# A recurrence on one core: the gates' passes cut differently, and a bias put into PSUM by ScalarE

## The reference, cut to what matters

```python
def cell(h, x):
    gi = x @ W_ih + b_ih
    gh = h @ W_hh + b_hh
    i_r, i_z, i_n = jnp.split(gi, 3, axis=-1)
    h_r, h_z, h_n = jnp.split(gh, 3, axis=-1)
    r = jax.nn.sigmoid(i_r + h_r)
    z = jax.nn.sigmoid(i_z + h_z)
    n = jnp.tanh(i_n + r * h_n)
    h_new = (1.0 - z) * n + z * h
    return (h_new, h_new)
hs = jax.lax.scan(cell, cond_2048, x)
```

## Time and profile before

| | us |
|---|---|
| median of 3 runs | 4225.12 |
| lowest, highest | 4210.37, 4236.23 |
| profiled execution, span (first to last instruction) | 4227.2 |
| TensorE (PE) busy | 3809.6 (90%) |
| TensorE weight load (PEld) busy | 2500.0 (59%) |
| VectorE (DVE) busy | 2336.6 (55%) |
| ScalarE (ACT) busy | 1317.9 (31%) |
| GpSimd (POOL) busy | 520.7 (12%) |

### The profile page before, as it was taken

One profiled execution on the slowest core, in us unless ns is written; L12 is line 12 of the kernel. 1 busy time (PEld: TensorE's weight loads), 2 busy tenths in 40 slices (PEclk: granted clock), 3 DMA queues, 4 the chain that ended last, 5 costly groups with the idle time before them and its releaser, 6 DMA issues. The chain is left out here.

```text
span 4227.2 us, 169699 instructions
## 1 busy us (share of the span) xinstructions
PE 3809.6 (90%) x68983; PEld 2500.0 (59%) x68983; DVE 2336.6 (55%) x6671; ACT 1317.9 (31%) x4227; POOL 520.7 (12%) x1107
## 2 busy tenths in 40 slices
PE   7999999999999999998899999689999979688880
PEld 3888888888888888886344343244333334344440
DVE  2555555555555555555677777444666654222226
ACT  0333333333333333332344444223444421011110
POOL 0010000100010000100222222000000004411110
PEclk9999999999999999999999999799999989898995
DMA  4900000000000000010111110101111212166677
GB/s 120 369 19 0 0 0 0 0 0 0 0 0 0 0 0 0 0 30 30 40 53 42 44 52 18 73 30 53 52 52 52 71 41 88 50 215 223 229 229 280
DMA packets 144030, 270.20 MB, mean 64 GB/s; under 512 B 23273, under 2 KB 70517, under 8 KB 140002
## 3 DMA queue, kind: packets, MB, share of 16 engines
q1 hardware_dynamic: 109570, 194.03, 13.7%
q10 hardware_dynamic: 20992, 57.17, 4.1%
q0 software_dynamic: 13408, 18.20, 1.2%
HBM read 148.41 MB, written 89.39 MB: 56 GB/s over the span
## 5 line engine op out<-in xcount | busy, mean ns | idle before, releaser
L310 PE MATMUL gru_pr<-ahead,h 128*4 128x128 f32 x16384 | 558.3, 274 | 14.2 <-DVE h L414 14.2
L310 PE MATMUL gru_pz<-ahead,h 128*4 128x128 f32 x16384 | 542.0, 273 | 4.2 <-issue 4.2
L310 PE MATMUL gru_pn<-ahead,h 128*32 128x128 f32 x16384 | 543.5, 273 | 0.0
L310 PEld LDWEIGHTS gru_pn<-ahead,h 128*32 128x32 f32 x16384 | 460.1, 110 | 1.4
L310 PEld LDWEIGHTS gru_pz<-ahead,h 128*4 128x4 f32 x16384 | 439.3, 87 | 12.0 <-issue 4.8
L310 PEld LDWEIGHTS gru_pr<-ahead,h 128*4 128x4 f32 x16384 | 342.1, 88 | 156.0 <-DVE h L414 25.7
L356 ACT ACTIVATE gru_rn<-gru_pre 128x16 f32<-128x16 f32 x512 | 120.2, 235 | 682.3 <-DVE gru_pre L396 682.3
L394 DVE STREAM_TRANSPOSE gru_tr<-gru_pr 128x128 f32<-128x128 f32 x512 | 162.1, 317 | 291.4 <-PE gru_pr L310 291.4
L927 DVE TENSOR_REDUCE da_mx<-da_ps 128x2 f32<-128x1024 f32 (+3 forms) x256 | 201.2, 817 | 131.9 <-PE da_ps L620 131.9
L273 POOL COPY gru_pick<-ident 128x4 f32 x512 | 96.0, 187 | 1445.5 <-PE gru_pz L301 1439.7
L407 DVE STREAM_TRANSPOSE gru_tz<-gru_pz 128x32 f32<-128x32 f32 (+1 forms) x1024 | 195.2, 229 | 122.9 <-PE gru_pz L310 122.9
(11 more groups left out here) (295 smaller groups left out, 5598.0 us busy)
## 6 DMA issues: line engine op xcount, KB each, us to landing
ahead<-in_L_ffn_gate_up_proj SPq DMA_DIRECT2D x64, 768.0 KB, 4.8
yk<-gru_zeros SPq DMA_DIRECT2D x6, 4096.0 KB, 34.8
ex_wd<-in_L_ffn_down_proj ACTq DMA_DIRECT2D x64, 384.0 KB, 6.3
xg<-gru_zeros SPq DMA_DIRECT2D x4, 4224.0 KB, 30.7
ex_xg<-xg ACTq DMA_DIRECT2D x64, 264.0 KB, 5.8
ahead<-wide SPq DMA_DIRECT2D x15, 1024.0 KB, 4.7
ahead<-xnT SPq DMA_DIRECT2D x15, 1024.0 KB, 4.5
co_got<-yk SPq DMA_DIRECT2D x8, 1536.0 KB, 7.9
```

What stands on the lines that cost most here:

```text
L310: last = nc.tensor.matmul(rows(j), of(c), whh[:, c, g, j, :], start=(c == 0 and start), stop=(c == KD - 1))
```

## The change

The same sums are made in another cut. Pass one ("rz") forms r's 128 columns of each group and the first 32 of z's, 160 in one matmul, into a new PSUM tensor `prz` that replaces `pr`; pass two forms n; pass three forms z's other 96 columns into `pz`. The 32 columns are z for the first quarter of h. W_hh is therefore laid out with the three gates side by side for each quarter and group, loaded by 64 DMAs in pieces of 128 values.

The order on TensorE becomes: rz for c = 0; n for c = 0; then the wait for the rest of h; rz for c = 1 to 3; n for c = 1 to 3; z. z's input is added by four matmuls of 32 columns and four of 96. All of the steps' matmuls have start off: they add to what `add_z_input` put there, to zero bits (r), or to n's bias.

n's bias is multiplied once, ahead of the loop, and kept as `bias_rows`; in each step ScalarE copies it into PSUM (`pn`) after `gru_tn` has been read and ahead of tanh, and TensorE's n waits for that (`seeded`). VectorE transposes 160 columns for r and the z quarter together; ScalarE does that quarter's sigmoid right after r's. The rest of z is one transposition of 96 columns and one sigmoid. The two scans for h stay, behind that transposition in VectorE's order.

```diff
--- before.py
+++ after.py
@@ -95,13 +95,14 @@
                 sp.wait_ge(xT_psum, (b - 1) * KD)
                 sp.dma_start(xin[:, b % 2, :, :], x[b].rearrange("(tt p) d -> p tt d", p=P)).then_inc(x_in[b % 2], 16)
             sp.wait_ge(w_spread, 3 * KD)
-            whh = t.ahead[:].rearrange("p (c g j f) -> p c g j f", c=KD, g=3, j=KD)
+            whh = t.ahead[:].rearrange("p (c j g f) -> p c j g f", c=KD, g=3, j=KD)
             for jj in range(KD):
-                rows = W_hh.rearrange("(jj c i) n -> jj i c n", jj=KD, c=KD)[jj]
+                rows = W_hh.rearrange("(jj c i) (g j f) -> jj i c j g f", jj=KD, c=KD, g=3, j=KD)[jj]
                 for c in range(KD):
-                    sp.dma_start(whh[32 * jj:32 * jj + 32, c, :, :, :].rearrange("i g j f -> i (g j f)"), rows[:, c, :]).then_inc(whh_in, 16)
+                    for j in range(KD):
+                        sp.dma_start(whh[32 * jj:32 * jj + 32, c, j, :, :], rows[:, c, j, :, :]).then_inc(whh_in, 16)
             sp.wait_ge(hin_in, 16 * KD * KD)
-            sp.wait_ge(whh_in, 16 * KD * KD)
+            sp.wait_ge(whh_in, 16 * KD * KD * KD)
 
         @block.gpsimd
         def _(pool):
@@ -201,18 +202,19 @@
         def sb(name, shape):
             return ctx.enter_context(nc.sbuf_tensor("gru_" + name, shape, F32))
 
-        whh = t.ahead[:].rearrange("p (c g j f) -> p c g j f", c=KD, g=3, j=KD)
+        whh = t.ahead[:].rearrange("p (c j n) -> p c j n", c=KD, j=KD)
+        RZ, Z, N = slice(0, P + 32), slice(P + 32, 2 * P), slice(2 * P, 3 * P)
         wih = t.ahead2[:].rearrange("p (k n) -> p k n", k=KD)
         xT = t.wide[:].rearrange("p (k b t) -> p k b t", b=B, k=KD)
         NG, NBL = 2 * KD, T // 32
-        bias, one = sb("bias", [P, KD, P]), sb("one", [P, 8 * B])
-        tr, pre = sb("tr", [P, KD, 32]), sb("pre", [P, ST])
-        tn, tz, narg = sb("tn", [P, KD * 32]), sb("tz", [P, KD, 32]), sb("narg", [P, ST, 4])
+        bias, one, bias_rows = sb("bias", [P, KD, P]), sb("one", [P, 8 * B]), sb("bias_rows", [P, P])
+        tr, pre = sb("tr", [P, KD + 1, 32]), sb("pre", [P, ST])
+        tn, tz, narg = sb("tn", [P, KD * 32]), sb("tz", [P, KD - 1, 32]), sb("narg", [P, ST, 4])
         rn, zin, pick = sb("rn", [P, ST, 4]), sb("zin", [P, D]), sb("pick", [P, 2, B])
         d0, d1 = sb("d0", [P, ST, 4]), sb("d1", [P, ST, 4])
         zeros = sb("zeros", [P, 1, XW])
-        pr = ctx.enter_context(nc.psum_tensor("gru_pr", [P, 4 * P], F32))
         pn = ctx.enter_context(nc.psum_tensor("gru_pn", [P, 4 * P], F32))
+        prz = ctx.enter_context(nc.psum_tensor("gru_prz", [P, 4 * P], F32))
         pz = ctx.enter_context(nc.psum_tensor("gru_pz", [P, 2, 4 * P], F32))
         pgi = ctx.enter_context(nc.psum_tensor("gru_pgi", [P, 4 * P], F32))
         wst = sb("wst", [P, KD, P])
@@ -224,6 +226,7 @@
         r_rows, n_rows, z_rows = sem("r_rows"), sem("n_rows"), sem("z_rows")
         tr_done, pre_done, r_act = sem("tr_done"), sem("pre_done"), sem("r_act")
         tn_done, gin_ready, set_up, bias_set = sem("tn_done"), sem("gin_ready"), sem("set_up"), sem("bias_set")
+        opened, seeded = sem("opened"), sem("seeded")
         narg_done, tanh_done, tz_done, z_act = (sem(n) for n in ("narg_done", "tanh_done", "tz_done", "z_act"))
         block = ctx.enter_context(nc.Block())
         state = t.h[:, :, 6]
@@ -289,33 +292,44 @@
         def _(pe):
             pe.wait_ge(loaded, 16)
 
-            def add_bias(s):
-                pe.wait_ge(tn_done, s * 1 + 1)
-                for j in range(KD):
-                    nc.tensor.matmul(pn[32 * j:32 * j + 32, 0:P], one[:], bias[:, j, :], start=True, stop=False)
+            pe.wait_ge(tn_done, 1)
+            for j in range(KD):
+                last = nc.tensor.matmul(pn[32 * j:32 * j + 32, 0:P], one[:], bias[:, j, :], start=True, stop=True)
+            last.then_inc(opened, 1)
 
             def add_z_input(s, par):
                 pe.wait_ge(pick_ready, s * 1 + 1)
-                pe.wait_ge(tz_done, s * 2 + 2)
+                pe.wait_ge(tr_done, s * 1 + 1)
                 for j in range(KD):
-                    last = nc.tensor.matmul(pz[32 * j:32 * j + B, par, 0:P], pick[:, par, :], zin[:, j * P:(j + 1) * P],
-                                            start=True, stop=False)
+                    nc.tensor.matmul(prz[32 * j:32 * j + B, P:P + 32], pick[:, par, :], zin[:, j * P:j * P + 32],
+                                     start=True, stop=True)
+                pe.wait_ge(tz_done, s * 1 + 1)
+                for j in range(KD):
+                    last = nc.tensor.matmul(pz[32 * j:32 * j + B, par, 0:P - 32], pick[:, par, :], zin[:, j * P + 32:(j + 1) * P],
+                                            start=True, stop=True)
                 last.then_inc(z_added, 1)
 
-            def gate(rows, g, of, start, done, s=None):
-                for c in range(KD):
-                    if s is not None and c < 2:
-                        pe.wait_ge(h_ready, s * 2 + (c + 1))
+            def part(rows, of, cols, cs, done=None):
+                for c in cs:
                     for j in range(KD):
-                        last = nc.tensor.matmul(rows(j), of(c), whh[:, c, g, j, :], start=(c == 0 and start), stop=(c == KD - 1))
-                last.then_inc(done, 1)
+                        last = nc.tensor.matmul(rows(j), of(c), whh[:, c, j, cols], start=False, stop=True,
+                                                skip_group_check=True)
+                if done is not None:
+                    last.then_inc(done, 1)
 
             def step(s, par):
                 after = lambda c: t.h[:, c * B:(c + 1) * B, 6]
                 places = lambda c: t.h[:, c * B:(c + 1) * B, :].rearrange("p b x -> p (b x)")
-                gate(lambda j: pr[32 * j:32 * j + B, 0:P], 0, after, True, r_rows, s)
-                gate(lambda j: pn[32 * j:32 * j + 32, 0:P], 2, places, False, n_rows)
-                gate(lambda j: pz[32 * j:32 * j + B, par, 0:P], 1, after, False, z_rows)
+                rz_rows = lambda j: prz[32 * j:32 * j + B, RZ]
+                n_of = lambda j: pn[32 * j:32 * j + 32, 0:P]
+                pe.wait_ge(h_ready, s * 2 + 1)
+                part(rz_rows, after, RZ, (0,))
+                pe.wait_ge(seeded, s * 1 + 1)
+                part(n_of, places, N, (0,))
+                pe.wait_ge(h_ready, s * 2 + 2)
+                part(rz_rows, after, RZ, (1, 2, 3), r_rows)
+                part(n_of, places, N, (1, 2, 3), n_rows)
+                part(lambda j: pz[32 * j:32 * j + B, par, 0:P - 32], after, Z, range(KD), z_rows)
 
             def next_gate_input(kb, c, k):
                 if k == 0:
@@ -331,14 +345,12 @@
                     for k in range(KD):
                         s = kb * 32 + c * KD + k
                         add_z_input(s, k % 2)
-                        add_bias(s)
                         next_gate_input(kb, c, k)
                         step(s, k % 2)
             with pe.Fori(T // 2 - 16, T // 2) as q:
                 for par in range(2):
                     s = q * 2 + par
                     add_z_input(s, par)
-                    add_bias(s)
                     step(s, par)
 
         @block.scalar
@@ -354,11 +366,13 @@
                 nc.scalar.activation(d0[:, :, 1], state, ACT.Copy).then_inc(h_copied, 1)
                 act.wait_ge(pre_done, s * 1 + 1)
                 nc.scalar.activation(rn[:, :, 2], pre[:], ACT.Sigmoid).then_inc(r_act, 1)
+                nc.scalar.activation(d1[:, 0:B, 2], tr[:, KD, 0:B], ACT.Sigmoid).then_inc(z_act, 1)
+                act.wait_ge(tn_done, s * 1 + 2)
+                nc.scalar.activation(pn[:, 0:P], bias_rows[:], ACT.Copy).then_inc(seeded, 1)
                 act.wait_ge(narg_done, s * 1 + 1)
                 nc.scalar.activation(d0[:, :, 2:4], narg[:, :, 3:4].broadcast_to([P, ST, 2]), ACT.Tanh).then_inc(tanh_done, 1)
-                for n, part in enumerate(PARTS):
-                    act.wait_ge(tz_done, s * 2 + (4 + n + 1))
-                    nc.scalar.activation(cb(d1[:, part.start * B:part.stop * B, 2]), tz[:, part, 0:B], ACT.Sigmoid).then_inc(z_act, 1)
+                act.wait_ge(tz_done, s * 1 + 3)
+                nc.scalar.activation(cb(d1[:, B:ST, 2]), tz[:, :, 0:B], ACT.Sigmoid).then_inc(z_act, 1)
 
             with act.Fori(0, NBL) as kb:
                 with act.Fori(0, 32) as n:
@@ -371,8 +385,8 @@
             dve.wait_ge(bias_set, 2)
             nc.vector.memset(one[0:1, 6:8 * B:8], 1.0).then_inc(bias_set, 1)
 
-            nc.vector.memset(pr[:], 0.0)
             nc.vector.memset(pn[:], 0.0)
+            nc.vector.memset(prz[:], 0.0)
             nc.vector.memset(pz[:], 0.0)
@@ -383,17 +397,21 @@
             nc.vector.memset(d1[:, :, 3], 1.0).then_inc(set_up, 1)
             dve.wait_ge(set_up, 6)
             dve.sem_inc(tn_done, 1)
-            dve.sem_inc(tz_done, 4)
+            dve.sem_inc(tz_done, 2)
+            dve.sem_inc(tr_done, 1)
```

(13 more changed lines are left out.)

## The result

The kernel after takes 4244.66 us (median of 9 runs, 4239.52 to 4252.03), the kernel before on the same chips 4226.39 (median of 9, 4210.37 to 4245.55). The ratio is 1.0035, 95% interval 1.0021 to 1.005: slightly slower, inside the 1% that the prediction called no change. The forecast was 4147, some 79 us faster; the kernel is 18 slower. The range (4102 to 4260) holds the time.

What follows compares the result with a forecast made beforehand. Each 3.64 us step was bound by z's chain, nearly tied with TensorE's tail. 392 steps x 0.21 = 82, less 120 x 0.03 = 4, gave about 79 us off: 4147, range 4102 to 4260.

Steps and rivals of the forecast that it cites:

- Part 4: z's 96 columns: rows at 2.81, first h scan at 3.18 after tanh and transposition, step 3.43, gain 0.21 us.
- Part 3: n's rows at 2.15, its transposition to 2.55, scan of tanh's argument at 2.59, tanh 2.91 to 3.15 us.
- What a record costs: Four-record TensorE waves follow a straight line in columns: 0.136 us for 160, 0.0825 for 96, 0.03 for 32.
- Rival A: TensorE's narrow waves do not shrink, so the change is slower: 4263 to 4302 us; chance 0.18.
- Part 1: rz first: TensorE has 0.49 us of work before needing the rest of h, so the 0.03 stall goes.
- Part 2: r's rows at 1.49 us instead of 1.09, their transposition to 1.91, r's sigmoid 2.27 to 2.50.
- Part 5: Rest of h reaches TensorE 0.33 us into the next step, under 0.49 of work: hidden.
- Part 6: Bias leaves TensorE's tail (2 waves, 0.22 us), z's input takes 4 waves; TensorE free at 3.35, under 3.43.
- Part 7: ScalarE's copy into PSUM ahead of tanh costs 0, since tanh could start at 2.84, under 2.91 us; 0.1 for the range.
- Part 9: Loading W_hh in 64 DMAs takes 32 us to issue, ending by 57, before the first step at 105.0.
- Part 8: The 120 steps after a loop's branch, held by TensorE's sequencer, take 3.67 us, a loss of 0.03 each.
- B: Another tie eats the gain, through costly 32-column input waves and late tanh: 4197 us; chance 0.22 with the rest of another rival.

Runs made afterwards that it cites:

- bias_multiplied: both_waits with n's bias multiplied on TensorE in every step and no ScalarE copy: 4223.95 us, 0.9996 of the kernel before.
- copy_one_column: both_waits with ScalarE's copy of n's bias cut to one of its 128 columns: 4148.85 us, 0.9824 of the kernel before.
- both_waits: Kernel after, first h scan waiting for tanh alone and tanh's argument scan carrying the wait for n's transposition: 4151.88 us, 0.9818 of the kernel before.
- value_first: Kernel after with tanh's wait moved behind that for z's first sigmoid, none dropped: 4211.39 us, 0.9969 of the kernel before.
- before_z_detached: Kernel before with an always fulfilled wait added ahead of the first h scan's wait for z's sigmoid: 4250.93 us, 1.005 of the kernel before.
- tensor_unrolled: both_waits with TensorE's inner loop over 8 steps instead of 4: 4504.71 us, 1.0661 of the kernel before.

## Why the prediction was wrong

The mechanism that it named for the gain is there. What failed is a term of the sum: two hand-overs on VectorE, in parts 4 and 3, were priced at 0.03 and 0.04, and measured 0.20 and 0.13.

- *What bounds the kernel before*: right. z's chain ended last and TensorE's tail all but tied with it; bias_multiplied shows the tie as soon as VectorE is quicker.
- *What a record costs*: right. By the line, 96 columns were to take 0.0825 a wave and 160 columns 0.136; z's 32 records take 0.84 less one record's 0.25 and the rest of its wave's 0.02, 0.57 for 7 waves, 0.082 each. The prediction's own sign, 0.66 for the 8 waves, came out too: z's first matmul starts at 1003.00, that of z's input at 1003.66. The four waves of z's input shrank too. The Trainium skill's 25 ns between starts of matmuls (TensorE: Matmul & The Clock Gate, "Wait — 56ns, not 53.3ns?") does not hold for the four records of a wave: at 0.10 a wave these 7 would have taken 0.70, and the two 32-column waves of z's input 0.20, where its 96-column matmuls start 0.06 behind them (1003.66 to 1003.72). Rival A fell with it.
- *Parts 1, 2, 5, 6, 7, 9*: right. h's rest came under the quarter's work, ScalarE's copy is free (copy_one_column), and the tail fits: 2.96 + 0.41 = 3.37 in both_waits, by L338's load at 1007.29, where 3.35 was forecast. W_hh's 64 DMAs took 43.88 us to issue and not 32, and were still done by 68.3, ahead of the first step. The timeline of SP's queue, kernel after:

```profile
24.43 43.88 SPq L103 DMA_DIRECT2D ahead<-in_L_cond_W_hh  x64
```

- *Part 3, the step that failed first*: "narg 2.59" came at 2.67. It took the distance from n's transposition to the scan, 0.03 to 0.04, from the step of the kernel before, where that wait was carried and r's sigmoid had ended 0.28 earlier. In the kernel after the wait is not carried, which gives 0.13. Even where it is again, the scan starts only after 0.06.
- *Part 4, the step that failed most*: "Scan of the first quarter after tanh and tz: 3.18" came at 3.42. It reckoned the scan as ready when its last input was, and priced the hand-over at that of a carried wait. That hand-over was measured in the kernel before on z's sigmoid; tanh, which now came last, had a wait of another kind. Measured: 0.20. Which of an instruction's waits is carried was never looked up, though the instructions for L410, L412 and L401 stood in the trace of before.
- *Part 8*: right in kind, 3.67 predicted; with the waits mended 3.69 in the rows above. In after it scarcely shows, since the ordinary steps take 3.67 too.
- *The sum*: with the two waits mended the kernel takes 4151.88 where 4147 was forecast for the change. So the rest of the sum holds within the noise (both_waits ran from 4144.84 to 4161.88), and the error is these two hand-overs: 3.67 less 3.44 in the ordinary steps, 0.23 or 0.24 x 392 = 90 to 94 us, and 4244.66 - 4151.88 = 93 by the times.
- *The rivals*: B ("a tie with something else eats the gain") is the nearest, but it named other ties and 4197. That tanh takes the place of z's sigmoid as the last was the thing to look for; the cost was not in the length of the wait but in its kind. The range held the time only because it was stretched over rivals B and A; the sum's own range, 4102 to 4186, did not.

## What to carry to other kernels

When a change turns round which of several inputs arrives last, or alters the values that the waits compare with, look at how the waiting instruction waits. By the rows of these kernels an instruction carries one wait; the others become instructions of the sequencer ahead of it. Against a carried wait, one that ends last there cost 0.07 us (value_first, before_z_detached), 0.10 where it was joined with another (L420), and 0.17 where a value for the next wait was reckoned behind it (L426, L428). The rows of all builds here fit one reading: a reckoning in the text puts the waits ahead of it into an instruction of their own, and of those left the first in the text is carried. So the input that comes last is written first, values are reckoned before it, and waits that an earlier one of the same engine implies are dropped. Ask the profile for the lines of the waits themselves: a row of the sequencer's at the line of the wait that ends last is the warning.

## What the runs showed of the hardware that was not expected

A longer loop body on TensorE made the kernel 6.6% slower than the one before, and 8.5% slower than both_waits. With 8 steps in the body instead of 4 the instruction queue moved 9.39 MB in 573 packets, where before, after and both_waits have 0.62 MB in 38. Over the 60 rounds that is 0.146 MB and 9 packets more a round. The row of that queue on the page of tensor_unrolled (packets, MB, share):

```profile
q8 instruction: 573, 9.39, 0.9%
```

TensorE then stands still once a round: in the stretch from 990 to 1090 us it is idle for 3.42, 3.55 and 3.86 us ahead of L304, some 34 us apart. It pays once more: after 3.55 us of idle the granted clock fell from 1.00, the 2.4 GHz level, to 0.50, that of 1.2, and the next step's rz loads took 1.43 where those at 1020.31, ahead of the stop, took 0.76. First the timeline of its loads:

```profile
1026.04 0.14 PEld L304 LDWEIGHTS gru_prz<-gru_zin,gru_pick 128*4 128x4 f32 x8 [3.55 <-issue]
...
1028.05 1.43 PEld L315 LDWEIGHTS gru_prz<-ahead,h 128*4 128x4 f32 x24
```

Then two windows of it, before and behind such a stop (the column behind the engines is the granted clock):

```profile
1020.00:1022.50 2.50, 2.50 (x96) 2.31 (x96) 1.50 (x6) 0.65 (x5) 0.61 (x1) 1.00 0.03 7
1027.40:1032.20 4.80, 4.80 (x93) 3.62 (x96) 1.13 (x4) 0.69 (x4) 0.00 (x0) 0.50 0.02 3
```

The recurrence grew by 365 us over both_waits (107.9 to 2280.6 against 108.4 to 1915.8, by the transpositions of r), 6.1 a round: the stop, and steps at the low clock behind it. That the body of 8 steps no longer fits some store and is fetched anew each round, as that of 4 is not, is an inference from the packets; the size of a store was not measured.
